# A moment's Newton steps kept in PSUM, and GpSimd's residual add placed between two half images

## The reference

```
x = x + L0(_gn(x));  x = x + L1(_gn(x))          # x: 32 images of 1024 tokens, 128 channels

def _L0(x, accumulators):                         # a softmax-weighted sum of exponentials, per position
    out = log(einsum('vhbk,vhks->vhbs', exp(x - x_max), exp(log_w - w_max))) + x_max + w_max

def _L1(x):                                       # attention of each image's tokens to one another
    nf = x / max(norm(x), 1e-12)
    A  = softmax(5 * (nf @ adj_w @ nf.T - rowmax))
    h  = A @ (x @ affine_w.T + affine_b)
    h  = (h - mean(h)) / sqrt(var(h) + 1e-5) * ln_g + ln_b      # over the 128 channels
    h  = where(h >= 0, h, 0.01 * h)
```

## Time and profile before

| | us |
|---|---|
| median of 3 runs | 1169.07 (1166.94 to 1171.18) |
| the profiled execution, total | 1164.44 |
| its span, first to last instruction | 1162.4 |
| TensorE busy | 1050.3 |
| VectorE busy | 935.0 |
| ScalarE busy | 929.6 |
| GpSimd busy | 573.4 |

### The profile page before, as it was taken

The page is one execution under the profiler, slowest core; times in us unless marked ns, Lnnn a source line. Parts: engine busy times, 40 slices in busy tenths (PEclk is TensorE's granted clock), DMA queues, the critical chain, the costliest instruction groups (busy, mean ns, idle before and its releaser), DMA issues.

```text
span 1162.4 us, 20953 instructions
## 1 busy us (share of the span) xinstructions
PE 1050.3 (90%) x7388; PEld 792.3 (68%) x7388; DVE 935.0 (80%) x1572; ACT 929.6 (80%) x1805; POOL 573.4 (49%) x395
## 2 busy tenths in 40 slices
PE   0199999659999999999999999999999999999992
PEld 0055555437777777777777777777777777777771
DVE  7823555677898988988799988989999989898873
ACT  0499999237888888888888888888888888888883
POOL 0045545312455555555555555565555555555534
PEclk9999999859999999999999999999999999999996
DMA  8889999610122222224322222222222222222222
GB/s 358 369 331 416 416 412 414 280 57 19 64 77 80 73 73 74 73 78 166 104 73 74 73 81 81 78 88 77 73 82 74 76 80 73 74 73 74 75 73 92
DMA packets 47355, 159.21 MB, mean 137 GB/s; under 512 B 5904, under 2 KB 6800, under 8 KB 37008
## 3 DMA queue, kind: packets, MB, share of 16 engines
q1 hardware_dynamic: 47248, 157.83, 36.2%
HBM read 137.50 MB, written 20.32 MB: 136 GB/s over the span
## 4 chain that ended last, share of the span: by engine, by line
PE 71%; DVE 15%; DMA 5%; ACT 3%; issue 3%; POOL 1%; SPq 0%; ACTq 0%; POOLq 0%; DVEq 0%
PE PS L1040 18%; PE PS L1042 17%; PE PS L1041 17%; PE PS L1058 5%; DMA Wt<-acc 5%; DVE st L636 4%; PE PS L1015 4%; DVE X L811 4%; PE PS L1005 3%; PE PS L1052 3%; DVE Pl L798 2%; PE PS L1026 2%; DVE X L809 2%; ACT PS L511 2%; PE PS L1046 2%
## 5 line engine op out<-in xcount | busy, mean ns | idle before, releaser
L798 DVE TENSOR_TENSOR Pl<-PS,Ph 128x512 fp32r<-128x512 f32 x512 | 339.5, 685 | 69.2 <-ACT PS L511 63.7
L511 ACT ACTIVATE PS<-PS 128x512 f32<-128x512 f32 x512 | 308.3, 603 | 12.1 <-PE PS L1042 8.9
L510 ACT ACTIVATE Ph<-PS 128x512 fp32r<-128x512 f32 x384 | 230.7, 601 | 104.5 <-PE PS L1042 100.2
L386 POOL TENSOR_TENSOR X<-X 128x512 f32<-128x512 f32 x64 | 85.2, 1331 | 350.3 <-DMA NU<-factor_rows 350.3
L1040 PE MATMUL PS<-Ph,hh 128*128 128x512 f32 x512 | 209.7, 410 | 1.5 <-DVE Pl L798 1.5
L1040 PE MATMUL PS<-uTh,nTh 128*128 128x512 f32 x512 | 200.7, 392 | 0.0
L1042 PE MATMUL PS<-uTh,nTl 128*128 128x512 f32 x512 | 200.3, 391 | 0.0
L1041 PE MATMUL PS<-Pl,hh 128*128 128x512 f32 x512 | 200.1, 391 | 0.0
L1041 PE MATMUL PS<-uTl,nTh 128*128 128x512 f32 x512 | 200.1, 391 | 0.0
L1042 PE MATMUL PS<-Ph,hl 128*128 128x512 f32 x512 | 199.9, 391 | 0.0
L360 POOL TENSOR_TENSOR LL<-LL 128x512 f32<-128x512 f32 x64 | 82.7, 1292 | 137.9 <-ACT LL L444 137.9
(11 more groups left out here) (106 smaller groups left out, 1784.4 us busy)
## 6 DMA issues: line engine op xcount, KB each, us to landing
Wt<-acc SPq DMA_DIRECT2D x64, 1024.0 KB, 7.4
X<-x SPq DMA_DIRECT2D x16, 1024.0 KB, 19.7
SQ<-norm_rows SPq DMA_DIRECT2D x32, 512.0 KB, 3.5
X<-factor_rows SPq DMA_DIRECT2D x64, 256.0 KB, 3.1
NU<-factor_rows SPq DMA_DIRECT2D x64, 256.0 KB, 3.6
out<-X SPq DMA_DIRECT2D x64, 256.0 KB, 2.0
out<-X SPq DMA_DIRECT2D x6, 512.0 KB, 4.7
X<-out SPq DMA_DIRECT2D x6, 512.0 KB, 6.5
```

The lines of the kernel that those rows point to most:

```text
L386: pool.tensor_tensor(fac_of(n), out_of(n), fac_of(n), ALU.mult).then_inc(output_weighted, 1)
L510: act.activation(Ph[:, g % RING, :], sl, ACT.Exp, scale=SHARP)
L511: act.activation(sl, sl, ACT.Exp, scale=SHARP).then_inc(weights_ready, 1)
L798: dve.tensor_tensor(Pl[:, r, :], SL[r], Ph[:, r, :].bitcast(F32), ALU.subtract)\
```

## The change

Three edits. Line numbers in the first column of `order` rows are the program's; behind the first edit the lines of the changed kernel are one or two lower (L809 is L808 there, L488 is L487).

```diff
 # GpSimd, pass b
-                    if b >= 2:
-                        add_residual(b - 2, 0)
+                    if b >= 2:
+                        add_residual(b - 2, 1)
                     if b + 1 < B:
                         unit_tokens(b + 1)
-                    if b >= 2:
-                        add_residual(b - 2, 1)
-                    if b + 1 < B:
                         values_lower(b + 1, 0)
                         tokens_lower(b + 1)
                         values_lower(b + 1, 1)
                     if 1 <= b <= B:
                         scale_output(b - 1, 0)
+
+                        add_residual(b - 1, 0)
                         scale_output(b - 1, 1)
 # ScalarE, pass b
                             if 1 <= b <= B:
                                 take_output(b - 1, 1)
                                 deviation_roots(b - 1, 0)
-                            if b + 1 < B:
-                                tokens_upper(b + 1)
                         if k == 4:
                             if b + 1 < B:
                                 values_upper(b + 1, 1)
+                                tokens_upper(b + 1)
 # VectorE, inverse_deviations
+                v = w[:, QH:2 * QH]
                 dve.wait_ge(q_roots, 2 * n + 2)
-                dve.scalar_tensor_tensor(out=qa, in0=w[:, QH:2 * QH], scalar=-0.5, in1=y, op0=ALU.mult,
+                dve.scalar_tensor_tensor(out=v, in0=v, scalar=-0.5, in1=y, op0=ALU.mult,
                                          op1=ALU.mult).then_inc(q_steps, 1)
-                dve.tensor_tensor(qa, qa, y, ALU.mult).then_inc(q_steps, 1)
+                dve.tensor_tensor(v, v, y, ALU.mult).then_inc(q_steps, 1)
-                dve.scalar_tensor_tensor(out=y, in0=qa, scalar=1.5, in1=y, op0=ALU.add,
+                dve.scalar_tensor_tensor(out=y, in0=v, scalar=1.5, in1=y, op0=ALU.add,
                                          op1=ALU.mult).then_inc(q_steps, 1)
```

## The result

| | before | after |
|---|---|---|
| median of the runs | 1168.01 (1166.75 to 1171.18, 4 runs) | 1149.25 (1148.57 to 1150.85, 4 runs) |
| the profiled execution, total | 1164.44 | 1148.57 |
| its span | 1162.4 | 1146.5 |

All times are in us. The ratio of the times is 0.9837, with a 95% interval of 0.9814 to 0.9861. The median before is that of four runs here and of three ahead of the forecast (1169.07). The changed kernel is 18.8 us faster between the medians and 15.9 us faster between the profiled executions. The forecast was 12.9 us and 1156.2 us. The sign and most of the place of the gain are as forecast, and the size is not: the kernel is 6.9 us faster than forecast, at the very low end of the range.

A forecast was written before the change was run, and what follows sets the result against it. TensorE sets the pace, waiting at the norms and queries: -12.7 - 2.7 + 2.5 lost at the end = -12.9 us, 1151.5 us profiled, 1156.2 us against the median; range 1149 to 1171 us.

The forecast's parts named there:

- The mechanism: VectorE instructions with two SBUF inputs wait for GpSimd's running instruction; with one PSUM input, L809 and L811 take 0.29 us.
- Rival C: PSUM doesn't free VectorE in the Newton step; half 1's stays slow, 2.7 us stay lost: about 1159 us, chance 0.09.
- The new wait: GpSimd waits for half 0's leaky function, so ScalarE's affine at k=0 starts 2.1 us late in every pass.
- the spare time: Between the Newton step's end and TensorE's norms, despite the late affine, about 0.55 us remain.
- rival B: GpSimd's hand-over isn't clean: affine 3.5 us late, 30 passes lose 0.4 us each, about 1181 us; chance 0.12.
- A: Affine 0.5 to 1.0 us later still, spare time gone, norms wait as before: about 1169 us, chance 0.13.
- The end: GpSimd's new order is unhidden in the last passes: 1.0 us at the last half's taking plus 1.5: 2.5 us lost.
- the step to the median: Forecast of 1151.5 us for the profiled execution, 4.6 below the median, was carried to 1156.2 us against median 1169.07.
- The norms: At k=7 TensorE's norms wait for half 0's Newton step, 29 waits; removing them was put at 12.7 us.
- The queries: TensorE's queries wait for VectorE's lower part of the queries, 3 waits; removing them was put at 2.7 us.
- Edit 3: ScalarE's tokens' rounding goes behind the exponentials of k=4, limiting the late affine's delay there to 0.2 us; costed at nothing.
- The rule on PSUM latency: PSUM source costs fixed 120 cycles against SBUF's 58; would make the three Newton steps an estimated 0.2 us longer.

The follow-up runs named there:

- the moves alone: Changed kernel with both halves' Newton steps back in SBUF, keeping GpSimd's new order and ScalarE's moved rounding: 1167.84 us, ratio 0.9985.
- second trace of before: The kernel before, run and profiled once more without an edit: 1169.58 us, ratio 1.0005.
- half 1 alone: Kernel before with only half 1's Newton step in PSUM: 1161.56 us, ratio 0.9932.
- half 0 alone: Kernel before with only half 0's Newton step in PSUM: 1163.55 us, ratio 0.9958.
- edit 1 alone: Kernel before with both halves' Newton steps in PSUM, GpSimd's and ScalarE's order as before: 1148.74 us, ratio 0.9801; again, 1150.04 us, ratio 0.983.

## Why the prediction came out as it did

**The mechanism was right.** A VectorE instruction with two SBUF inputs is held until GpSimd's instruction ends, and one with a PSUM input is not: L808 and L810 show it in all 64 cases each, and the kernel with the moves alone shows the other side. "SBUF — State Buffer" of the Trainium skill, section "Who interferes with whom", says the same in general: an instruction of VectorE with two SBUF inputs contends with a GpSimd instruction that reads SBUF, one with at most one doesn't (outside the modes that use both ports), and the lock is exclusive. The trace agrees: 0.29 us against up to 1.39 for L811. Rival C (PSUM doesn't free VectorE) is out.

**The new wait and the spare time were right.** The prediction put the affine of half 1 2.1 us late in every pass. One pass of the changed kernel, GpSimd, VectorE and ScalarE:

```profile
798.88 1.28 POOL L394 TENSOR_TENSOR X<-X 128x512 f32<-128x512 f32 x1 [6.74 <-DVE X L818]
800.12 1.29 POOL L386 TENSOR_TENSOR X<-X 128x512 f32<-128x512 f32 x1
801.49 1.29 POOL L388 TENSOR_TENSOR X<-X,NU 128x512 f32<-128x512 f32 x1
...
798.11 0.69 DVE L818 SCALAR_TENSOR_TENSOR X<-X 128x512 f32<-128x512 f32 x1
...
802.81 0.82 ACT L539 ACTIVATE X<-X,lbc,gcol 128x512 f32<-128x512 f32 x1 [1.96 <-POOL X L388]
```

The affine starts 18.1 us behind the norms ahead of it (784.71), where it was at 16.0 to 16.2 in most passes before: 2.0 us late, with a wait of 1.96 us. The leaky takes 0.69 us and each GpSimd step 1.28 or 1.29, so the hand-over is clean and rival B is out. It is absorbed, so A is out too. At k=4 ScalarE's order is the one worked out:

```profile
808.01 0.58 ACT L509 ACTIVATE Ph<-PS 128x512 fp32r<-128x512 f32 x1
...
809.52 1.05 ACT L487 ACTIVATE nTh<-SQ 128x1024 fp32r<-128x1024 f32 x1
```

The spare time was put at 0.55 us and measured 0.64 in three ways.

**The end was right.** Worked out as 2.5 us, it measured 2.4 in the profile.

**The forecast failed in two steps.** The first is the step to the median, which carried a distance of 4.6 us over as if it were fixed: it makes 4.0 of the 6.9 us. The second is the size of the terms for the passes, -15.4 us where -18.4 were measured between the profiled executions (16.9 in the 28 passes and 1.5 ahead of them): it makes the other 3.0. In the sum's own terms:

- *The norms.* I took 12.7, the middle between the idle time in the list and the steps from start to start. The 29 waits were worth about 13.3: an ordinary pass went from 27.51 to 27.09 us, 28 times with the pass ahead of the first norms, and the long one from 28.45. This lies between my 12.7 and the 14.0 of the steps from start to start, so this term was nearly right. What an engine loses is the distance between starts: 0.43 us a pass here, for 0.34 to 0.39 us of idle time in the list. There was no reason for a middle, and that it came near is luck.
- *The queries.* I took the 2.7 us of idle time. The three passes with such a wait took 28.66 to 28.69 us where their neighbours take 27.50: about 1.17 us each, 3.5 in all, for 0.9 us of idle time.
- *The number of those waits.* I read 3 from the profiled execution, which is faster than each of the four runs behind the median of before, and then carried the sum over to the median, which lay 4.6 us above it, as if the distance were the same in the changed kernel. The second trace of before has 7. They come and go between executions of one kernel: the step of half 1 is late enough only where GpSimd's scaling and centring cover both of its middle instructions. VectorE in the pass of the earlier trace rows before:

```profile
469.10 1.37 DVE L809 TENSOR_TENSOR X<-X 128x128 f32<-128x128 f32 x1
470.51 1.34 DVE L811 SCALAR_TENSOR_TENSOR X<-X 128x128 f32<-128x128 f32 x1
...
472.69 0.68 DVE L777 TENSOR_TENSOR uTl<-PS,uTh 128x512 fp32r<-128x512 f32 x1
```

  Here both are held, by 1.08 and 1.05 us. When GpSimd starts depends on when the rows land from memory. In the changed kernel neither instruction is held, there are none of these waits, and its profiled execution lies 0.7 us below its median and not 3.6. This makes the 2.9 us between 15.9 and 18.8. That the runs without a profile have more of the waits than the 3 is argued: from the second trace, from the 7 to 8 us of half 1 alone, and from the spread (9.6 us over the ten runs of the kernel before, 4.7 over the ten with half 1's step in PSUM). Those runs leave no record of their waits.
- *Edit 3.* The sum had no term for it, and the working costed the moved rounding at nothing. It gained 1.0 us in pass 0, where it keeps GpSimd away from L694, an instruction that the prediction didn't look at.
- *The rest.* Four passes before were 0.1 to 0.3 us longer than the usual, about 0.5 us in all, which no term covers.
- *The sum as a sum.* The norms' and the queries' waits stood as two terms. The kernels with one half in PSUM show that they hang together: with half 0's step repaired alone, the queries' waits grow from 3 or 7 to 13. That the sum came out at all for this change is because edit 1 repairs both. A prediction for half 0 alone by the same sum would have promised 12.7 us, and 5 were there.

**The rule on PSUM latency** of the Trainium skill ("VectorE: DVE Perf Modes"), which the prediction set against the row of L814, gives an estimated 0.2 us for the whole Newton step. The four instructions start 0.32, 0.33 and 0.33 us apart and take 1.27 us, where the prediction said about 1.3: L814's row decides, and the rule's difference doesn't appear for these 128x128 tiles.

## What to carry to other kernels

Where VectorE and GpSimd work side by side, look for VectorE lines whose median duration is a multiple of their minimum; if such a line is on the critical path, give it one input in PSUM, in a bank that is there anyway, and don't count on a new order of GpSimd for it: here that order moved the hold-up onto the next step. Look at the small instructions too, with their longest duration and not the median alone: L694 was held once, and moving one ScalarE instruction freed it. Cost a wait by the distance between the starts of what waits, in a pass with it and one without, not by the idle time in a list. Before waits that come and go by chance are put into a sum, look at a second execution, and ask of each repair whose work it will move onto the next step.

## What the runs showed of the hardware that was not expected

- Writing PSUM from VectorE, which no row of before showed, costs next to nothing: 299 ns with one input and the output in PSUM (L808), 291 ns with the output in SBUF (L810).
- The hold-up isn't proportional. A held 128x128 instruction took 0.58 to 1.42 us for 0.29 in the two traces of before, according to how much of GpSimd's instruction was left, and one of 128x28 took 2.13 for 0.18.
- The time from the start of the span to the loop's first exponential differs by up to 3.7 us between executions of kernels that do the same there (257.7 to 261.4). What makes it differ was not tried.
- In the pass behind the one in which the spilled images come back, 0 to 1.8 us are lost in the kernels without other waits: 27.12 us in the changed kernel's first trace, 27.93 in its second, 28.89 in one of edit 1 alone. The rows land 10 to 12 us behind the norms in that pass instead of 5. Between the norms of pass 1 and of pass 29 it is the one place where TensorE still waits in these kernels, and it was left open.
